# Gate and output projection of an RWKV block: a deeper software pipeline, another VectorE order, and the root as exp(-ln/2)

## The reference, cut to what matters

```
r    = sigmoid(Wr @ groupnorm(x2))          # x2: what enters the block
y    = 0.5 * (y_forward + y_backward)       # the two WKV scans
h    = r * y
h    = (h - mean(h)) / sqrt(var(h) + 1e-5)  # over the 192 channels
x3   = x2 + Wo @ (h * ln_g + ln_b)
stat = per-channel statistics of x3         # for the next group norm
```

## Time and profile before

| what | value |
|---|---|
| median of 3 runs | 14534.5 us (14530.72 to 14544.68) |
| profiled execution | 14526.16 us, its span 14524.4 us |
| PE busy over the span | 13173.8 us (91%) |
| ACT, DVE, POOL busy | 11848.2, 11475.4, 7260.6 us |
| first DMA issue of the stage | 10524.94 us |
| first instruction of the next phase | 11148.94 us |

### The profile page before, as it was taken

How to read it: one execution, slowest core, us unless ns; L and a number is a source line. 1 busy time by engine, 2 the same in 40 slices (tenths; PEclk the granted TensorE clock), 3 DMA queues, 4 the chain that set the end, 5 groups by cost and what they waited for, 6 DMA issues and landing times. The chain is left out here.

```text
span 14524.4 us, 244913 instructions
## 1 busy us (share of the span) xinstructions
PE 13173.8 (91%) x80556; PEld 10401.7 (72%) x80556; DVE 11475.4 (79%) x14230; ACT 11848.2 (82%) x17113; POOL 7260.6 (50%) x3802
## 2 busy tenths in 40 slices
PE   7899999999999999999999997667077989999999
PEld 3699999999999999999999997223022335555555
DVE  4588887788878887877888786578966988888888
ACT  2599999999999999999999996119644879999998
POOL 0155555555555555555555554053310018888887
PEclk9999999999999999999999998568587889999999
DMA  4466666666666666666666667434332443333333
GB/s 107 123 171 169 171 170 169 171 171 171 170 170 172 170 171 169 172 168 170 170 171 171 170 171 161 105 87 154 122 104 76 154 138 103 102 102 102 102 102 90
DMA packets 825516, 2100.02 MB, mean 145 GB/s; under 512 B 82811, under 2 KB 439473, under 8 KB 681009
## 3 DMA queue, kind: packets, MB, share of 16 engines
q1 hardware_dynamic: 814289, 2070.18, 54.4%
q10 hardware_dynamic: 9984, 14.16, 0.3%
HBM read 1815.36 MB, written 268.74 MB: 143 GB/s over the span
## 5 line engine op out<-in xcount | busy, mean ns | idle before, releaser
L524 PE MATMUL dc_p<-dc_t 96*128 96x144 f32 x51912 | 6892.8, 286 | 30.0 <-PEq L521 29.5
L584 POOL TENSOR_TENSOR dc_t<-dc_t 128x648 f32<-128x648 f32 x2884 | 4614.4, 1600 | 4374.0 <-POOLq L583 4374.0
L524 PEld LDWEIGHTS dc_p<-dc_t 96*128 96x128 f32 x51912 | 6522.6, 189 | 75.8 <-issue 53.7
L625 DVE TENSOR_TENSOR dc_t<-dc_p,dc_t 128x1296 f32<-128x1296 f32 x2884 | 4343.7, 1506 | 987.3 <-DVEq L623 971.7
L463 ACT ACTIVATE dc_t<-dc_t 96x1152 f32<-96x1152 f32 x2886 | 3595.7, 1246 | 113.7 <-ACTq L462 111.6
L465 ACT ACTIVATE dc_t<-dc_t 96x1152 f32<-96x1152 f32 x2886 | 3360.3, 1164 | 365.1 <-ACTq L464 16.0
L1985 DVE TENSOR_TENSOR_SCAN ms_t<-ms_t,ms_p 128x512 f32<-128x512 f32 x1728 | 2128.0, 1271 | 283.0 <-PE ms_p L1927 203.5
L1901 POOL TENSOR_TENSOR ms_t<-ms_t 128x1536 f32<-128x1536 f32 x576 | 1988.0, 3457 | 503.2 <-DVE ms_t L1985 499.3
L640 DVE TENSOR_TENSOR dc_t<-dc_t 128x324 f32<-128x324 f32 x2883 | 1427.6, 495 | 684.4 <-DVEq L638 645.8
L1937 PE MATMUL ms_p<-ms_t,top_t 128*128 128x512 f32 x3456 | 1775.0, 596 | 0.0
L561 PE MATMUL dc_p<-dc_t 128*128 128x180 f32 (+1 forms) x7488 | 1655.4, 321 | 68.4 <-PEq L556 49.7
(11 more groups left out here) (206 smaller groups left out, 10090.1 us busy)
## 6 DMA issues: line engine op xcount, KB each, us to landing
dc_t<-sxd SPq DMA_DIRECT2D x1443, 864.0 KB, 5.8
ms_t<-bcd SPq DMA_DIRECT2D x576, 256.0 KB, 3.3
dc_t<-xrT SPq DMA_DIRECT2D x145, 675.0 KB, 5.7
kvd<-wk_t SPq DMA_DIRECT2D x18, 1536.0 KB, 5.1
xvd<-mi_t SPq DMA_DIRECT2D x36, 768.0 KB, 3.5
szd<-mi_t SPq DMA_DIRECT2D x36, 768.0 KB, 5.7
dld<-mi_t SPq DMA_DIRECT2D x36, 768.0 KB, 3.4
ms_t<-dld SPq DMA_DIRECT2D x36, 768.0 KB, 6.8
```

Of the source, the lines that this page charges most:

```text
L524: ins = e.matmul(PT[j % 2][:, t // 3, (t % 3) * 144:(t % 3 + 1) * 144], HX[:, m % NHX, t * 128:(t + 1) * 128], XW[:, i, ky:ky + WIN, g * C ...
L584: e.tensor_tensor(z[:, :, 0:HALF], z[:, :, 0:HALF], z[:, :, HALF:2 * HALF], ALU.add)\
L625: e.tensor_tensor(Zt[:, n % 4, :].rearrange("p (b m i) -> p b m i", b=3, i=CG), PT[n % 2][:, :, 0:432].rearrange("p b (m i) -> p b m i", i ...
```

## The change

Only `gate_and_project` is changed. The steps and their tiles stay the same, apart from the root. What is different:

- Order and distance. DVE's iteration i is now scale(i-3), gate(i), put(i-4), centre(i-1), statistics(i-4). ACT's is norm(i+1), Sigmoid(i), affine(i-3), Square(i-1), root(i-2). PE's is PR(i), PO(i-4), PM(i-1), PV(i-2). The loops run N + 4 times.
- The root. DVE's add of eps and its reciprocal, and ACT's Sqrt, go. ACT does Ln with eps as bias (from PSUM PV) and Exp with scale -0.5. An explicit table load of a set that holds both stands ahead of them.
- Buffers: XI 9 slots (was 6), YF and YB 4 (was 6), HH 5 (was 3), RS 3 and HN 3 (were 2).
- Semaphores count up to N and are waited for by their value; a new block at the end waits for the totals and takes them down. The `tick` memset (L64) and the separate release of the constants (s_wr) are gone.
- SP loads three chunks ahead (four in flight), waits for gate(i-1) ahead of YF and YB, and stores chunk i-6 in iteration i. SP no longer waits for the constants ahead of the first loads.

```diff
-    R = 6
+    RX, RY, R2 = 9, 4, 2
...
-                e.wait_ge(s_w, 64).then_inc(s_w, -64)
...
+                    if n >= RX:
+                        e.wait_ge(s_xo, n - RX + 1)
+                    e.dma_start(XI[:, n % RX, :, :], k.d["x2"][b, :, :, t0:t0 + T].rearrange("h p n -> p h n"))\
+                        .then_inc(s_xi[n % RX], 16)
+                    if n >= RY:
+                        e.wait_ge(s_h, n - RY + 1)
...
+                for i in range(N + 6):
+                    if i + 3 < N:
+                        load(i + 3)
+                    n = i - 6
...
+                def spread(n):
+                    e.wait_ge(s_var, n + 1)
+                    if n >= 3:
+                        e.wait_ge(s_hn, n - 2)
+                    e.activation(RS[:, n % 3, :], PV[n % 2][:, :], ACT.Ln, bias=EP[:, 0:1]).then_inc(s_ln, 1)
+                    e.wait_ge(s_ln, n + 1)
+                    e.activation(RS[:, n % 3, :], RS[:, n % 3, :], ACT.Exp, scale=-0.5).then_inc(s_rs, 1)
...
+                for i in range(N + 4):
+                    if i + 1 < N:
+                        norm(i + 1)
+                    if i < N:
+                        sigmoid(i)
+                    if 3 <= i < N + 3:
+                        affine(i - 3)
+                    if 1 <= i <= N:
+                        square(i - 1)
+                    if 2 <= i < N + 2:
+                        e.preload_act_table_set("natural_log_exp_and_others")
+                        spread(i - 2)
...
+                for i in range(N + 4):
+                    if i < N:
+                        e.wait_ge(s_xn, i + 1)
+                        if i >= 1:
+                            e.wait_ge(s_sg, i)
+                        project(PR, WR, XN[:, i % R2]).then_inc(s_r, 1)
+                    if 4 <= i:
+                        n = i - 4
+                        e.wait_ge(s_af, n + 1)
+                        if n >= 1:
+                            e.wait_ge(s_xo, n)
+                        project(PO, WO, HN[:, n % 3]).then_inc(s_po, 1)
...
-                        e.reciprocal(RS[:, q, :], RS[:, q, :]).then_inc(s_v, 1)
...
+                for i in range(N + 4):
+                    if 3 <= i < N + 3:
+                        scale(i - 3)
+                    if i < N:
+                        gate(i)
+                    if 4 <= i:
+                        put(i - 4)
+                    if 1 <= i <= N:
+                        centre(i - 1)
+                    if 4 <= i:
+                        statistics(i - 4)
...
+        with p.block() as blk:
+            @blk.sync
+            def _(e):
+                for s, total in ((s_w, 64), (s_xn, N), (s_r, N), (s_sg, N), (s_s, N), (s_h, N), (s_m, N), (s_d, N),
```

More of the change, by code:

```diff
@@ L1362, in _ @@
-                for n in range(5):
+                        e.dma_start(Y_[:, n % RY, :, :], src[b, :, :, u0:u0 + T].rearrange("h p n -> p h n"))\
+                            .then_inc(s_yy[n % RY], 16)
+                for n in range(3):
                     load(n)
[L1364 to L1370, removed]
@@ L1383, in norm @@
                                            bias=GN[:, 2 * b + h, 1:2], scale=GN[:, 2 * b + h, 0:1])
                     ins.then_inc(s_xn, 1)
-                norm(0)
[L1387 to L1404, removed]
@@ new lines, in sigmoid, with square @@
+                def sigmoid(n):
+                    e.wait_ge(s_r, n + 1)
+                    if n >= R2:
+                        e.wait_ge(s_h, n - R2 + 1)
+                    e.activation(SG[:, n % R2, :, :], PR[:, :, :], ACT.Sigmoid).then_inc(s_sg, 1)
+                def square(n):
+                    e.wait_ge(s_d, n + 1)
+                    if n >= R2:
+                        e.wait_ge(s_var, n - R2 + 1)
+                    e.activation(SQ[:, n % R2, :, :], HH[:, n % 5, :, :], ACT.Square).then_inc(s_sq, 1)
@@ new lines, in spread, with affine @@
+                def spread(n):
[5 more added lines that the diff above has]
+                    e.activation(RS[:, n % 3, :], RS[:, n % 3, :], ACT.Exp, scale=-0.5).then_inc(s_rs, 1)
+                def affine(n):
+                    e.wait_ge(s_hn, n + 1)
+                    for h in range(2):
+                        ins = e.activation(HN[:, n % 3, h, :], HN[:, n % 3, h, :], ACT.Identity,
+                                           bias=GB[:, h, 1:2], scale=GB[:, h, 0:1])
+                    ins.then_inc(s_af, 1)
@@ L1424, in _ @@
[L1424 to L1437, removed]
+                    return ins
@@ L1485, in _, with put, statistics @@
-                e.wait_ge(s_pof, 1).then_inc(s_pof, -1)
+                e.memset(EP[:, :], EPS).then_inc(s_ep, 1)
+                def put(n):
+                    q = n % R2
+                    e.wait_ge(s_po, n + 1)
+                    if n >= R2:
+                        e.wait_ge(s_st[q], 16 * (n // R2))
+                    e.tensor_tensor(XO[:, q, :, :], PO[:, :, :], XI[:, n % RX, :, :], ALU.add).then_inc(s_xo, 1)
+                def statistics(n):
+                    e.wait_ge(s_xo, n + 1)
+                    for m in range(2):
+                        ins = e.bn_stats(k.ST2[:, 2 * (n // NCH) + m, n % NCH, :], XO[:, n % R2, m, :])
+                    ins.then_inc(s_bn, 1)
```

143 lines of the change are left out of this document (69 added, 74 removed).

## The result

| | before | after |
|---|---|---|
| median of the runs | 14534.24 us (14530.72 to 14544.68, 4 runs) | 14329.14 us (14320.13 to 14347.12, 4 runs) |
| profiled execution | 14526.16 us | 14329.85 us |
| stage, first DMA issue to the next phase | 624.0 us | 423.6 us |

The ratio is 0.9859, 95% interval 0.9842 to 0.9876: 1.4% faster, 205 us by the medians and 196 by the two profiled executions. 14,348 us was forecast, with a range from 14,328 to 14,405; the measured time is 19 us lower and lies 1 us above the lower end.

What follows compares the result with a forecast made beforehand. No engine was full, so a chain through several engines was taken as the bound. Savings of 148 us in the loop, 15 and 3 at the start, 22 at the end, less 2.5, gave 14,348 us, range 14,328 to 14,405.

Steps and rivals of the forecast that it cites:

- The chain: New loop: Sigmoid, gate, put, centre, Square, load, Ln, Exp, norm, load and Sigmoid again, 11.3 us an iteration.
- TensorE next, with a gap and no loss of clock: In the loop, 24 TensorE instructions take 10.3 us, leaving a gap of about 1.0 us at full clock.
- the one early gap of 0.94 us: Early in the old stage, TensorE's instructions behind this gap ran at full clock, so no clock loss was forecast.
- Rival A: In the loop, TensorE's clock drops each iteration and its 12.9 us become the bound: 50 us, 14,398; chance 0.08.
- The add over the scale: GpSimd's add starts near 5.5 us behind the gate's end, runs over VectorE's scale and is gone before the next gate.
- Rival B: In the loop, GpSimd's add falls on the gate every time: 1.5 us, 31 times, 46 us, 14,395; chance 0.08.
- Rival C: ScalarE's table switches cost twice, a load's length added to each: 80 us over the loop, 14,428; chance 0.03.
- The start: Up to the first Sigmoid: earlier loads save 1.8 us, the first table load not waiting for PR 1.3; 12.9 us.
- the fill: First four iterations: 6.5 and 7.5 us, then 10.2 each; 34 us, bounds 31 and 38.
- the last part: From the last Sigmoid, the last chunk passes four more iterations without Sigmoid, gate and norm: 34 us, bounds 30 and 40.
- The close: Stage's end: 3.4 us plus 0 to 5, taken as 2.5, for the new block's 33 waits and barrier; 5.9 us.
- its own terms: The range's lower end, 14,328: short bounds of start, end and Exp (3 + 4 + 6) and a little of the close.

Runs made afterwards that it cites:

- root_only: The kernel before with Ln (eps as bias) and Exp replacing add of eps, Sqrt and reciprocal, old order kept; 14365.8 us, ratio 0.9902 to before.
- y_late: The changed kernel with SP issuing XI and the store ahead of YF and YB; 14320.5 us, ratio 0.9872 to before.
- two_loads_more: The changed kernel with two more table loads per iteration between Square and Ln; 14414.4 us, ratio 0.9931 to before.
- order_only: The changed kernel with the old root: Sqrt on ScalarE and the reciprocal on VectorE ahead of the scale; 14325.2 us, ratio 0.9868 to before.
- one_load_more: The changed kernel with one more table load per iteration between Square and Ln; 14366.5 us, ratio 0.9899 to before.
- centre_less_pe: The changed kernel with centre ahead of put and one of the variance average's two matmuls left out (not computing the reference); 14283.5 us, ratio 0.9837 to before.

## Why the prediction was right, point by point

**The chain.** Right, and shown. Its members are those summed: taking put out took its 1.14 us out until TensorE stopped it, a load more put 1.29 in, and the chain without put came out at 9.94 against 9.93. Its sum of 11.31 was 0.23 us longer than the step of 11.08. The steps that differ, read from the rows above: gate 1.12 behind Sigmoid (1.16), centre to Square 1.24 (1.33), Exp 0.71 behind Ln (0.78), norm to load 1.52 (1.54), and 0.01 less from Exp to norm; Ln itself, at 0.68, was longer than the 0.63 taken. The three largest go with the old code's waits, which also take the semaphore down and from whose rows the forecast took its steps: root_only has these waits, and there the three steps are 1.16, 1.33 (10783.91 to 10785.24) and 0.80 us. No run changes the waits alone. If it is the waits, a part of the change to which the forecast gave no price is worth some 0.2 us in each step, about 6 us in the loop.

**TensorE next, with a gap and no loss of clock.** Right. The gap was 0.56 us where 1.0 was forecast: 0.23 because the step was shorter, and 0.2 because the forecast counted 10.3 us from start to start, while the 24 instructions behind a gap take 10.52 to the end of the last (10806.02 to 10816.54). The clock is 1.00. The argument from the one early gap of 0.94 us held, and the runs show how far: no slow instructions stood behind the gaps up to 1.54 us in the loops of y_late, root_only and two_loads_more. They did behind one gap of 1.64 us in order_only, behind 11 of 15 gaps of 1.85 in one_load_more, and behind every gap of 3.15. Rival A did not occur. Its price, 50 us for 12.9 us of work, was never tested with TensorE as the bound.

**The add over the scale.** Right: 5.2 us from issue to add (near 5.5 was taken), the scale held to 2.32, the gate free in the loop. Once, in the fourth step of the stage, the add did fall on the gate (2.79 us). Rival B's mechanism was made to act by y_late and cost 5.6 us of stage, since its add, 7.3 to 8.6 us behind the issue, only just reaches the gate.

**Table switches.** Rival C did not occur: Square at 10798.42, load at 10799.50, Ln at 10800.79, all at once behind each other. The rule of the Trainium skill (ScalarE: Activation LUTs, "What ACT_TABLE_LOAD costs") with a drain of 1.38 us beside each load isn't borne out for switches between instructions that follow at once: an added load cost 1.29 us in the period, not 2.66.

**Start, fill and last part.** These were sized less well than the loop. The start gave 2.1 us where 3.1 was forecast. The two gains named came as forecast: the first load of XI is issued 1.85 us earlier behind the stage's start, and the first Sigmoid no longer waits for a table load behind PR (1.36 us). Two losses weren't in it: the first norm began 3.84 us behind its load's issue in before and 4.39 now, and the first PR took 6.01 us in place of 5.47. Why is open; the loads of the constants were still in flight now, and had landed before. In the fill the first two steps took 4.85 and 6.19 us where 14.0 was assumed for both, and the fourth took 11.52 because its gate was held; the errors partly cancel, and that the part came out at 32.5 for 34 is in so far luck. Of the 2.5 us by which the last part was shorter, 0.6 lie ahead of the last centre's end and 1.6 between the end of the last Square and that of its Exp.

**The close.** The new block of 33 waits and its barrier were put at 2.5 us and cost nothing that shows (3.37 against 3.44). The traces show where it went. In both kernels the last store lands 0.36 us ahead of the next phase's first instruction (10949.04 and 11148.58), so the close is that landing. The new block asks for the stores last, and its other waits pass while they land. The WKV phase, from which the bound was taken, waits for its stores already at the end of its loop, ahead of the block, so all waits of that block come behind the landing: in before its last store lands at 10513.53, and the next phase begins 3.38 us behind that. That the order of the waits makes the difference is argued from the code; no run moves them.

**The number and the range.** The stage was forecast at 438 us (437.8 by its parts) and took 423.6, which is 14.2 us less: 8.7 of them in the loop, 2.5 each in the last part and the close, 1.5 in the fill, less 1.0 at the start. The rest of the 19 us lies outside the stage: 9.0 us come from how the medians lie to the profiled executions (8.3 above it in before, 0.7 below it in after), which is chance, and 4.1 us went the other way (see below). The lower end of the range is also not what its own terms give: 3 + 4 + 6 us and 2.5 of the close reach from 14,348 down to some 14,332, and the measured 14,329 lies below that. That it is inside 14,328 is luck; that it is a gain of about this size is not.

**What was not in the prediction.** That either half of the change alone would bring most of the gain. The prediction followed the whole change only. The sums for the halves (11.3 and 11.5) took some steps from the trace of after; with the steps of before they would have been 11.4 and 11.7, so they could have been made then. And 4.1 us of the stage's gain are not in the profiled execution's 196.3. The stage started 0.9 us later. Behind it the next phase's group norm now has a table load of its own (1.28 us, since Ln and Exp were the last set in use), so that its first image load comes 13.4 us behind the stage's end where it was 12.2. What follows that load took 2.1 us more, which is within the spread of the nine profiled executions (3362.2 to 3367.2 us).

## What to carry to other kernels

When no engine of a loop is full, write down the chain that closes on itself in each engine's order, start to start, and ask of each member whether it must lie there: a step that nobody in the chain needs, as put here, costs its length by its place alone. Two remedies for one chain do not add up; work each out alone, then see which engine is next, for that is where the gain ends (here 10.3 us of TensorE). A slow instruction costs almost nothing once the order gives it a place beside another engine's share of the chain: the 3.35 us reciprocal of order_only made a step of 11.12 us against 11.08, and cost more only where the pipeline empties. A wait for a store's landing is best put last; the close here came out as the landing and nothing more, though that is argued and not tested.

## What the runs showed of the hardware

- An add on GpSimd held VectorE's gate and its scale (both inputs in SBUF) until about 1.1 us behind the add's end (2.32 and 1.72 us in place of 1.22, and 2.83 in the earlier trace rows). The reciprocal, with one input, ran its 3.35 us beside such an add in order_only (10788.49 to 10790.84) without loss.
- The hold goes both ways. In centre_less_pe the scale and the add start almost together: where the scale started at 10773.99 and the add 0.11 us behind it, the scale took 1.22 us and the add 3.32 in place of 2.35; where the add started at 10793.86 and the scale 0.02 behind it, the add took 2.36 and the scale 3.42.
- TensorE's granted clock was 1.00 with a gap of 0.56 us in each step of 11.08 us (after) and with gaps of mostly 1.14 in 11.77 (root_only). It was 0.93 in steps of 12.37, most with a gap of 1.85, the others with one of 0.16 to 0.6 behind slow instructions; 0.94 with gaps of 3.15 and 1.45 by turns in 13.65; and 0.82 with gaps of 2.6 to 4 us in 16.1.
- Of four transfers of 384 KB issued together, GpSimd's add waited for the last two in y_late and started 7.3 to 8.6 us (7.7 on average) behind the first issue; in after it waited for the first two and started 4.9 to 5.4 us (5.1) behind it. They landed in the order of issue throughout the loop (108 transfers in after, 103 in y_late), so the order in which SP lists them was worth 2.6 us to whoever waits.
